# Cross-attention scores and maxima by pairs of heads in 64-row tiles of TensorE

## What is computed

```
q = (h @ Wq + bq).reshape(B, 56, 16, 8)          # B = 16
k, v = (c @ Wk + bk), (c @ Wv + bv)              # c: (B, 1500, 128), reshaped to 16 heads of 8
scores = einsum('bqhd,bkhd->bhqk', q, k) / sqrt(8)
attn = softmax(scores, axis=-1)                  # over 1500
out = einsum('bhqk,bkhd->bqhd', attn, v)         # then @ Wo + bo, added to x
```

## Time and profile before

| | us |
|---|---|
| median of 3 runs | 2073.19 (2069.59 to 2075.86) |
| the profiled execution | 2065.48 |
| its span | 2063.6 |
| PE busy | 1729.7 (84%) |
| DVE busy | 1261.6 (61%) |
| ACT busy | 994.5 (48%) |

### The profile page before, as it was taken

The page is one execution under the profiler, slowest core; times in us unless marked ns, Lnnn a source line. Parts: engine busy times, 40 slices in busy tenths (PEclk is TensorE's granted clock), DMA queues, the critical chain, the costliest instruction groups (busy, mean ns, idle before and its releaser), DMA issues.

```text
span 2063.6 us, 49011 instructions
## 1 busy us (share of the span) xinstructions
PE 1729.7 (84%) x18191; PEld 1152.2 (56%) x18191; DVE 1261.6 (61%) x2445; ACT 994.5 (48%) x1875; POOL 406.5 (20%) x609
## 2 busy tenths in 40 slices
PE   6888877699999988784899999997785889999986
PEld 4565534366666665442566666664342666666663
DVE  3455343577777774454777777772555777777762
ACT  1344232266666664332465666663231556666652
POOL 4000422033333313243033333300230000000000
PEclk9799978599999998796799999998885899999998
DMA  5121011332222221021322223220022233322210
GB/s 174 46 75 70 20 37 38 70 90 83 84 84 82 81 65 50 9 67 31 78 84 86 85 82 84 80 79 1 6 71 53 65 88 88 88 83 84 69 41 10
DMA packets 116117, 137.24 MB, mean 67 GB/s; under 512 B 60063, under 2 KB 106466, under 8 KB 116002
## 3 DMA queue, kind: packets, MB, share of 16 engines
q1 hardware_dynamic: 114418, 134.58, 22.9%
q10 hardware_dynamic: 1008, 1.05, 0.2%
q0 software_dynamic: 576, 0.02, 0.0%
HBM read 55.03 MB, written 0.46 MB: 27 GB/s over the span
## 4 chain that ended last, share of the span: by engine, by line
PE 63%; DVE 12%; issue 8%; SPq 7%; ACT 6%; DMA 3%; POOL 1%; DVEq 0%; ACTq 0%; POOLq 0%
PE PS L1069 10%; PE PS L1093 8%; PE PS L1119 8%; PE PS L987 6%; PE PS L993 6%; PE PS L833 6%; SPq L408 6%; DVE mx L1528 3%; PE PS L912 3%; PE PS L1202 2%; PE PS L982 2%; PE PS L930 2%; DMA k_st<-k_lo 2%; ACT k_hi L704 2%; PE PS L903 1%
## 5 line engine op out<-in xcount | busy, mean ns | idle before, releaser
L1528 DVE TENSOR_REDUCE mx<-PS 112x1 f32<-112x500 f32 x1152 | 715.3, 671 | 203.9 <-PE PS L1069 201.2
L768 ACT ACTIVATE q_parts<-PS 125x448 f32<-125x448 f32 x1152 | 555.8, 544 | 271.2 <-PE PS L1119 269.7
L1069 PE MATMUL PS<-k_st,q_mx 96*112 96x500 f16 x1152 | 436.8, 409 | 86.0 <-DMA q_mx<-q_all 44.5
L564 POOL TENSOR_SCALAR cx<-cx,norm_b 125x128 f32<-125x128 f32 x384 | 303.1, 812 | 586.7 <-DMA cx<-in_ctx 456.9
L1119 PE MATMUL PS<-q_st,k_st 98*125 98x224 f16 x2304 | 326.3, 264 | 22.6 <-ACT q_parts L768 21.1
L1119 PEld LDWEIGHTS PS<-q_st,k_st 98*125 98x125 f16 x2304 | 260.8, 137 | 118.0 <-ACT q_parts L768 60.1
L1093 PE MATMUL PS<-q_parts,v_sb 125*18 125x112 f32 x9216 | 293.9, 261 | 2.3 <-ACT q_parts L768 1.3
L1069 PEld LDWEIGHTS PS<-k_st,q_mx 96*112 96x112 f16 x1152 | 144.3, 132 | 211.0 <-issue 122.3
L1093 PEld LDWEIGHTS PS<-q_parts,v_sb 125*18 125x18 f32 x9216 | 209.1, 98 | 76.2 <-ACT q_parts L768 47.8
L708 ACT ACTIVATE v_sb<-PS 125x512 f32<-125x512 f32 x144 | 87.0, 604 | 257.2 <-PE PS L993 253.7
L1435 DVE SCALAR_TENSOR_TENSOR k_lo<-PS,vec,k_hi 128x500 f16<-128x500 f32 x144 | 106.2, 737 | 97.2 <-ACT k_hi L704 97.2
(11 more groups left out here) (262 smaller groups left out, 1940.6 us busy)
## 6 DMA issues: line engine op xcount, KB each, us to landing
cx<-in_ctx SPq DMA_DIRECT2D x56, 750.0 KB
k_st<-k_hi SPq DMA_DIRECT2D x384, 62.5 KB, 2.4
k_st<-k_hi SPq DMA_DIRECT2D x384, 31.2 KB, 1.9
k_st<-k_lo SPq DMA_DIRECT2D x192, 62.5 KB, 2.0
q_mx<-q_all SPq DMA_DIRECT2D x48, 168.0 KB, 2.7
q_st<-q_all SPq DMA_DIRECT2D x48, 168.0 KB, 2.7
q_all<-q_parts SPq DMA_DIRECT2D x36, 196.0 KB, 4.1
v_sb<-in_ctx SPq DMA_DIRECT2D x8, 750.0 KB
```

The source lines that it names most:

```text
L564: last = pool.tensor_scalar(cx[:, p, c, :], cx[:, p, c, :], norm_b[:, p, 0, c:c + 1], norm_b[:, p, 1, c:c + 1], ALU.subtract, ALU.mult)
L768: act.activation(probs[:, c % RING, u * HR:(u + 1) * HR], PS[0:KC, (2 * c + u) % SC_RING, 0:HR], ACT.Exp).then_inc(sem("exp_done"), 1)
L1069: mm(PS[0:PW, MX_BANK + u % MX_RING, 0:TK], q_mx[0:96, p, rb // 2, (rb % 2) * PW:(rb % 2) * PW + PW], k_st[0:96, p, rb // 2, TK * t:TK * t ...
L1528: dve.tensor_reduce(mx[:, rb, t:t + 1], PS[0:PW, MX_BANK + u % MX_RING, 0:TK], AX.X, ALU.max)\
```

## The change

**Tiles.** Scores and maxima no longer work on groups of four heads in 98 or 96 rows but on pairs of heads in ROWS = 2 + 3 x 16 = 50 rows, at partition 0 or at partition 64 (a = 0 or 1), with k = 0 to 3 for the four pairs of each half. Rows 0 and 1 of each tile are for the maximum, then 16 rows each of k_hi, k_hi and k_lo (for Q: high, low, high). A score matmul has 112 columns and not 224; there are eight for each chunk, alternating between the two tiles and into two banks. A unit is still 112 queries by 500 keys; consecutive units alternate between the tiles. In each slot PE now issues two units ahead of the preparation step and only a third behind it.

**Layout through DRAM.** Q and K are written to DRAM (`k_out`: 2 DMAs for each 500 keys) and read back into the two tiles (`k_in`: 6 DMAs). K goes in three pieces of 500 keys, each waiting only for the scores that last read its columns. SP's order in `attend` changes with it. The mask has two columns and not four, so the masked Q of lines 753 and 1515 takes half the instructions and half the space.

**Shift.** The eight small matmuls write rows 0 to 1 and 64 to 65 of one bank; DVE casts one half (2 x 448), ACT copies the other (`shift_rows`). Scores and the next units wait for both.

**Elsewhere.** Layer 0's scores buffer `p0` lies in `A_first` and no longer in `k_st`. POOL clears all of `q_all` and writes ones to two rows of `k_st` twice, in place of one memset of 32 rows; it does so before the first `qk_copy`, as before. Some semaphores are merged.

```diff
-ROWS = 98
+QUAD = 4
+ROWS = 2 + 3 * 2 * DH
-PIECES = ((0, TK), (TK, S))
-PIECE_OF = (0, 1, 1)
+PARTS = (0, 0, 1)
+Q_PART_OF = (0, 1, 0)
...
+        def ge_known(eng, *waits):
+            values = [(name, v if isinstance(v, int) else eng.to_reg(v)) for name, v in waits]
+            eng.wait_ge(sem("ident_done"), 1)
+            for name, v in values:
+                ge(eng, name, v)
...
+                def k_out(batch, t):
+                    b, i, p = batch
+                    n = n0 + b
+                    ge_known(sp, (f"k_stacked{t}", STACKED * n), ("k_lo_done", NT * n + t + 1))
+                    for part, src in enumerate((k_hi, k_lo)):
+                        sp.dma_start(k_dram[part, :, TK * t:TK * t + TK], src[:, TK * t:TK * t + TK])\
+                          .then_inc(sem(f"k_out{t}"), 16)
+                def k_in(batch, t):
+                    b, i, p = batch
+                    n = n0 + b
+                    free = 0 if isinstance(b, int) and b < 2 else 2 * C * (n - 2) + 2 * TC * (t + 1)
+                    ge_known(sp, ("scores_ready", free), (f"k_out{t}", 32 * (n + 1)))
+                    for a in range(2):
+                        for k, part in enumerate(PARTS):
+                            r = 64 * a + 2 + 2 * DH * k
+                            sp.dma_start(k_st[r:r + 2 * DH, p, :, TK * t:TK * t + TK],
+                                         k_dram[part, 64 * a:64 * a + 64, TK * t:TK * t + TK]
+                                         .rearrange("(k d) s -> d k s", k=QUAD)).then_inc(sem(f"k_stacked{t}"), 16)
...
                 def attend(batch, following, behind, third):
                     if following:
+                        if not start:
+                            k_in(following, 2)
                         q_scores(following)
                     if behind:
-                        q_max(behind)
-                        stack(behind, 0)
                         if not (isinstance(b, int) and b + 4 >= B):
                             load((b + 4, i + 2, p))
-                        stack(behind, 1)
+                        k_out(behind, 0)
+                        k_out(behind, 1)
+                        k_in(behind, 0)
+                        k_out(behind, 2)
+                        k_in(behind, 1)
+                        q_max(behind)
...
-                    mm(PS[0:PW, MX_BANK + u % MX_RING, 0:TK], q_mx[0:96, p, rb // 2, (rb % 2) * PW:(rb % 2) * PW + PW],
-                       k_st[0:96, p, rb // 2, TK * t:TK * t + TK], start=True, stop=True).then_inc(sem("max_ready"), 1)
+                    mm(PS[0:PW, MX_BANK + u % MX_RING, 0:TK], q_mx[64 * a:64 * a + ROWS, p, k, :],
+                       k_st[64 * a:64 * a + ROWS, p, k, TK * t:TK * t + TK], start=True, stop=True)\
+                        .then_inc(sem("max_ready"), 1)
...
-                    for u in range(2):
-                        ge(pe, "exp_done", 2 * n + u + 1 - SC_RING)
-                        for g in range(2 * u, 2 * u + 2):
-                            last = mm(PS[0:KC, (2 * c + u) % SC_RING, (g % 2) * GW:(g % 2) * GW + GW],
-                                      k_st[0:ROWS, p, g, c * KC:(c + 1) * KC], q_st[0:ROWS, p, g, :], start=True, stop=True)
-                        last.then_inc(sem("scores_ready"), 1)
+                    ge(pe, "exp_done", 2 * n + 2 - SC_RING)
+                    for k in range(QUAD):
+                        for a in range(2):
+                            last = mm(PS[0:KC, (2 * c + a) % SC_RING, k * PW:k * PW + PW],
+                                      k_st[64 * a:64 * a + ROWS, p, k, c * KC:(c + 1) * KC],
+                                      q_st[64 * a:64 * a + ROWS, p, k, :], start=True, stop=True)
+                            if k == QUAD - 1:
+                                last.then_inc(sem("scores_ready"), 1)
...
-                        if tiles:
-                            unit(following, tiles.pop(0))
+                        for t in tiles[:2]:
+                            unit(following, t)
...
-                        for t in tiles:
+                        for t in tiles[2:]:
                             unit(following, t)
...
-                    dve.tensor_copy(q_st[96:ROWS, p, :, :].rearrange("p (u g) n -> p u (g n)", u=2),
-                                    PS[96:ROWS, MX_BANK:MX_BANK + 2, 0:HR]).then_inc(sem("shift_done"), 1)
+                    dve.tensor_copy(q_st[0:2, p, :, :].rearrange("p k n -> p (k n)"), PS[0:2, MX_BANK, 0:QUAD * PW])\
+                       .then_inc(sem("shift_done"), 1)
```

More of the change, by code:

```diff
@@ L411, in _ @@
                 load((0, 0, 0))
                 load((1, 0, 1))
-                stack((0, 0, 0), 0)
-                load((2, 1, 0))
-                stack((0, 0, 0), 1)
-                stack((1, 0, 1), 0)
-                load((3, 1, 1))
-                stack((1, 0, 1), 1)
+                for b in range(2):
+                    for t in range(NT):
+                        k_out((b, 0, b), t)
+                    load((b + 2, 1, b))
+                    for t in range(NT):
+                        k_in((b, 0, b), t)
```

136 lines of the change are left out of this document (70 added, 66 removed).

## The result

The changed kernel takes **2185.9 us** (median of 4 runs, 2175.6 to 2197.1) against 2071.4 (4 runs): ratio 1.056, 95% interval 1.048 to 1.063. The forecast was 2059 with a range of 1985 to 2108. The profiled execution took 2197.05 us, span 2195.3; that of before 2065.48. The first is the slowest of its four, so the 131.7 us between the two spans, which the next paragraphs divide, are 17 more than the 114.5 between the medians.

The account below looks back on a forecast made before the run. PE was taken to bound the kernel (busy 84% of the span), partly through waits in loops with other engines. 2065.5 + 0 - 12 - 2 = 2051.5, plus 7.7 for the median of runs, gave 2059 us, range 1985 to 2108.

Parts of the forecast that it names:

- Terms 1 and 2: Scores, then units, side by side in two row tiles: -2.0 and -2.1 us of PE array time a period.
- Term 3: More changes between 64-row and full-array work on PE, with longer first matmuls after them: +2.3 us a period.
- The steady period stays: Mid-layer loops: two periods take 53.25 us for 53.23, within about 0.5 us a period either way.
- The walk: One period followed slot by slot through PE, DVE and ACT: 26.1 us for 25.78; joining batch 27.15 for 27.45.
- rival B: Pairs of units stall on DVE's banks in several slots: +0.5 us a period, 2081 us; chance 0.15.
- SP's queue: q_mx, now issued last on SP, comes at 24.8 us of the period, needed at 26: hidden by about 1 us.
- rival C: q_mx comes late because k_in and k_out issues cost 0.59 + 0.04 us: period 27.6, total 2101 us; chance 0.12.
- At nothing: POOL's memsets: Kernel start: POOL's memsets end at 37.6 us, before the first copy at 42.04, so they cost nothing.
- Term 4: K in three pieces shortens units' waits for keys in layers' first and last periods: -12 us (0 to -36).
- Term 5: Layer starts: fewer masked-Q instructions and SP issues, and a shorter first shift: together -2 us.

Follow-up runs that it names:

- the split wait: Score matmuls tile after tile, each tile with its own wait: on the three edits 2101.7 us, ratio 1.0157; alone on the changed kernel 2217.3 us, 1.072.
- filler: The three edits plus six 128-row matmuls of nothing behind each chunk's scores in the last batch of each layer: 2062.5 us, ratio 0.9977.
- the three edits: Changed kernel with one unit ahead, q_mx behind the first six k_in, and POOL's memsets as float32, the ones in one piece: 2075.9 us, ratio 1.0031.
- whole rows: The three edits with units and scores over rows 0 to 113 at once, summing two heads' scores: 2100.8 us, ratio 1.0161.
- narrow filler: The three edits plus six matmuls of nothing, 50 rows each, behind each chunk's scores in the last batches: 2083.6 us, ratio 1.0066.

## Why the prediction was wrong, by its own steps

**Terms 1 and 2, right.** Two row tiles overlap. A chunk's scores cost 0.27 us for the 0.39 of before (I had 0.22), so -1.4 and not -2.0; a pair of units costs 0.31 up to the transposes, the change of tiling included.

**Term 3, right in kind.** 0.10 us is left between a pair of units and the transposes, where I took 0.09. My sum is a little off in itself (14.5 x 0.09 is 1.3, not 1.4). With units in full-array form and scores in tiles a period is 0.5 to 1.0 longer, but there units also no longer run beside scores. PE's busy time in two periods fell by 2.9 us, I had 3.6.

**"The steady period stays", wrong: 55.4 for 53.2 in two.** The walk said K1 ends 0.2 earlier, and the loss comes in slot 7. The rows show K1 starting 0.7 later already, with 0.75 for 0.33 of waiting for an exponential in the second chunk, and the chain K2, `k_hi`, `k_lo`, V0 goes late by 1.5. I had looked for the cost of a pair in slot 7 alone; the run with pairs in slots 0 to 5 shows 0.6 us of it in the early slots. As I read it, a pair behind the one or two units of the slot before asks for three or four banks of a ring of three, and PE stands ahead of the preparation step. One unit ahead brings back 1.0 and 1.1 (25.95 and 27.23), the whole excess. The merged wait, which stays there, is worth 0.2 and 0.1 (25.75 and 27.12 with the split wait). It is rival B in mechanism, priced at 0.5 for some 1.1 a period: by my estimate 42 x 1.1 = 46 us of the 98 of the loops.

**SP's queue, wrong by 3.0 us in the period shown.** I summed 8.5 us from K1's `k_lo` to the start of the issue of `q_mx` (16 issues, the waits of registers). The trace has 1146.5 to 1158.0 = 11.5: the sum left out that SP stands for 2.6 us until K0's data are in DRAM before it can read them back, and six `k_in` took 3.90 there for 2.71 elsewhere; the rest went 0.8 faster than I had it. From that start to the first unit it is 3.4 us and not 2.9. The margin was 1 us, the unit came 2.57 late. It is rival C's effect by another price than C's: an issue of a `k_in` costs about 0.45, as I had it.

**What no term had: TensorE's clock.** Every step was priced at the full clock of the earlier trace rows. The kernel before keeps it in its loops but for 35 us; the changed one loses it in mid-layer, behind waits for `q_mx` of up to 3 us (92 us) and in places where PE never waits longer than 1.05 us (48 us), in the first period of each layer as before, and in the last batches. Shown: taking the late `q_mx` away takes 100 us of half clock in the profiled executions and 37 us off the median; gaps put into the kernel before make 150 us of half clock; filler turns a last batch of 20.6 us into 16.9. What sets off the 48 us isn't shown; with one unit ahead and `q_mx` early most of them are gone. The Trainium skill ("TensorE: Matmul & The Clock Gate", Loop structure matters more than you think) warns of long DMA waits between matmuls for this reason. The traces agree in kind: 2.57 us of waiting for `q_mx` up to 1161.46, and half clock from 1163.0. The loops' other 52 us are such waits and what follows them, since the three edits bring the loops back to 1200.9 us; no run divides waits from clock. Of the last batches' 17.7 us filler brings back some 9; the other 8 stay, nearly all at full clock.

**"At nothing: POOL's memsets", wrong: the first transposes start 15.2 us later, the first unit 13.4.** I asked whether POOL would be done before its own next instruction. DVE was what waited, and I read past a sign of it: in the kernel before, the same cast took 2.53 us, to the end of POOL's memset. The Trainium skill ("SBUF — State Buffer", SBUF: two separate sides) has the rule: DVE in some of its modes and POOL share one pair of ports, which one of them holds for its whole instruction. The runs agree: the cast starts at 18.7, 18.3 and 18.0 in three kernels and ends when the memset does, after 8.93, 9.41 and, with the short memsets, 1.72 us.

**Term 4 held**, as far as it shows: the waits for `k_st`, 36.7 us, are gone. Term 5's sign holds: from the projection of Q to the landing of the first `q_mx` 10.6 us for 13.4. Neither can be told apart in the total.

**The best version.** Three edits and filler give 2062.5 us, ratio 0.9977 (0.9953 to 1.0002): at best 0.5% faster than before, at worst equal. The change's gain on the array is in it, and what it buys is close to nothing: PE is busy for 46.4 us in two periods where it was 49.4, and the two take 53.2 us as before. So PE's array time no longer sets the period; as I read it, the loops through ACT and DVE do. That the forecast had 53.25 too is no hit, since it was for a kernel with pairs of units ahead.

**Open:** why some iterations load code again and let PE stand still, most of them with the split wait; what brings half clock where no wait is longer than 1.05 us; whether rows or tiling made the narrow filler fail; how the merged wait costs the kernel before 1.1%; why the last batches at full clock still take 16.9 us with filler and 17.7 with whole rows, for 14.6.

## What to carry to other kernels

Price a step that makes TensorE idle, or its matmuls narrow, twice: once for itself, and once for the time that follows at half clock; and when single fixes look worthless, try them together, since each may only pay once the clock holds. Between a write to DRAM and its reading back count the landing, on the queue that waits. Before a memset of POOL is called hidden, look at what DVE does beside it.

## What was not expected of the hardware

- Matmuls of different row tiles overlap whatever their order in the program: eight in 0.44 us, alternating or four and four, at full clock.
- With filler of 50 rows PE was busy for 22.3 of 23.7 us at a mean clock of 0.58; with filler of 128 rows for 14.8 of 16.9 at 1.00.
- A cast of 128 elements in each partition by DVE took 8.93 and 9.41 us beside memsets of POOL, and ended when they did.
- POOL's memset takes as long for 2 partitions as for 128 (10.1 us for 12000 elements), and half as long for the same bytes as float32 (5.10).
- A write of 125 KB to DRAM, issued at 1144.31, could be read back only at 1150.00, 5.7 us later; the six issues of the reading took 2.7 to 3.9 us.
- PE stood still for 3.0 to 4.5 us at the head of 13 iterations of the loop, those in which the queue of instructions moved some nine packets of 16 KB where others moved none or one, and 6.8 to 23.9 us at half clock followed.
